# First stage of a transformer layer: buffers for h's rows, later weight parts, table products on GpSimd, and more summed z

## The reference, cut to what matters

```python
dt = jnp.exp(log_dt)
dt_Lambda = dt[:, None, 0] * Lambda[None, :, 0] + 1j * (dt[:, None, 1] * Lambda[None, :, 1])
pos = jnp.arange(L, dtype=jnp.float32)            # L = 1024
...
num = jnp.exp(dt_Lambda_neg) - 1
den = jnp.exp(dt_Lambda_neg * L) - 1
Wc = Wc * num * _reciprocal(den * Lam, EPS)       # Wc is x, as complex numbers
P = dt_Lambda[..., None] * pos - P_max[..., None]
K = jnp.einsum('chn,hnl->chl', Wc, jnp.exp(P))
return K.real.astype(jnp.float32)
...
h = _L0_tok_ref(L0_tok_log_dt, L0_tok_Lambda, x, 1024)
h = h + _L0_attn_ref(_layernorm(h, axis=-1), L0_attn_Wq, L0_attn_Wk, L0_attn_Wv, L0_attn_Wo)
h = h + _L0_ffn_ref(_layernorm(h, axis=-1), L0_ffn_A, L0_ffn_B, L0_ffn_Wr, L0_ffn_br)
```

## Time and profile before

| | |
|---|---|
| time, median of 3 runs | 2504.96 us (2502.73 to 2509.3) |
| the profiled execution's own time | 2504.22 us, span 2502.4 us |
| first stage, its first matmul to its last | 42.06 to 294.94 us |
| TensorE busy over the span | 2349.1 us (94%) |
| VectorE, ScalarE, GpSimd busy over the span | 1952.3, 1850.1, 1629.6 us |
| second stage, from its first load | 300.40 us to the end |

### The profile page before, as it was taken

One profiled execution on the slowest core, in us unless ns is written; L12 is line 12 of the kernel. 1 busy time (PEld: TensorE's weight loads), 2 busy tenths in 40 slices (PEclk: granted clock), 3 DMA queues, 4 the chain that ended last, 5 costly groups with the idle time before them and its releaser, 6 DMA issues.

```text
span 2502.4 us, 58994 instructions
## 1 busy us (share of the span) xinstructions
PE 2349.1 (94%) x18752; PEld 1245.7 (50%) x18752; DVE 1952.3 (78%) x7939; ACT 1850.1 (74%) x6398; POOL 1629.6 (65%) x1508
## 2 busy tenths in 40 slices
PE   2888679999999999999999999999999999999986
PEld 2677534444455544454455454444555545444543
DVE  8888547888788778788787778788887778887864
ACT  5777547777777777777777777777777777777773
POOL 1233147777777777777777777777777777777772
PEclk9999889999999999999999999999999999999997
DMA  2777559999999999999999999999999999999984
GB/s 74 215 210 213 166 103 167 176 184 184 182 186 188 183 177 179 186 185 184 181 188 186 185 174 181 185 185 184 184 187 184 179 181 182 184 186 186 182 164 101
DMA packets 1199527, 443.66 MB, mean 177 GB/s; under 512 B 1149552, under 2 KB 1151856, under 8 KB 1199216
## 3 DMA queue, kind: packets, MB, share of 16 engines
q1 hardware_dynamic: 1199216, 439.89, 88.9%
HBM read 87.42 MB, written 67.11 MB: 62 GB/s over the span
## 4 chain that ended last, share of the span: by engine, by line
PE 69%; DVE 13%; issue 2%; ACT 2%; POOL 1%; DMA 1%; POOLq 0%; DVEq 0%; ACTq 0%
PE pb L817 8%; PE pb L819 7%; PE pb L818 7%; PE pa L817 6%; PE pa L818 6%; PE pa L819 6%; PE pv_ps L846 4%; PE pc L817 4%; PE pc L818 4%; PE pc L819 4%; PE s_ps L831 4%; DVE pr L1111 2%; DVE bn L1130 2%; DVE h L1221 2%; DVE nrm L1144 2%
## 5 line engine op out<-in xcount | busy, mean ns | idle before, releaser
L968 ACT ACTIVATE pr<-pr,smin 128x128 f32<-128x128 f32 x2048 | 792.8, 389 | 111.5 <-DVE smin L1111 111.3
L1325 POOL TENSOR_TENSOR p<-pr,p 128x512 f16<-128x512 f32 x512 | 600.8, 1174 | 254.1 <-ACT p L978 244.0
L1317 POOL TENSOR_TENSOR pr<-pr,rinv 128x512 f32<-128x512 f32 x512 | 529.7, 1040 | 268.2 <-DVE rinv L1119 268.2
L978 ACT ACTIVATE p<-pr 128x512 f16<-128x512 f32 x512 | 319.6, 624 | 238.5 <-POOL pr L1317 218.6
L1111 DVE CUSTOM_DVE_ANT_0 pr<-s_ps,cst 128x128 f32<-128x128 f32 x2048 | 470.3, 284 | 27.0 <-POOL p L1325 13.9
L968 ACT ACTIVATION_READ_ACCUMULATOR pr<-pr,smin 128x1 f32 x2048 | 383.6, 187 | 0.0
L576 PE MATMUL hps<-z,xw 128*128 128x256 f32 x896 | 214.5, 402 | 80.4 <-POOL xw L304 42.1
L576 PEld LDWEIGHTS hps<-z,xw 128*128 128x128 f32 x896 | 179.8, 203 | 114.7 <-issue 45.8
L831 PEld LDWEIGHTS s_ps<-kt,qt 128*128 128x128 f16 x2048 | 152.7, 98 | 145.3 <-DVE smin L1111 45.4
L1165 DVE TENSOR_TENSOR xs<-h_ln,xs 128x512 f16<-128x512 f32 x128 | 123.7, 968 | 125.1 <-ACT xs L1013 125.1
L817 PE MATMUL pa<-wkv_hi,xt 128*128 128x512 f16 x512 | 197.2, 385 | 25.0 <-DMA xt<-xs 25.0
(11 more groups left out here) (189 smaller groups left out, 5747.1 us busy)
## 6 DMA issues: line engine op xcount, KB each, us to landing
h<-hout SPq DMA_DIRECT2D x128, 256.0 KB, 3.3
h_ln<-h SPq DMA_DIRECT2D x64, 512.0 KB, 4.3
h_res<-h SPq DMA_DIRECT2D x64, 512.0 KB, 4.7
out<-h SPq DMA_DIRECT2D x64, 512.0 KB, 5.4
pt<-p SPq DMA_TRANSPOSE x512, 3.3
xa<-x SPq DMA_DIRECT2D x16, 256.0 KB, 4.7
xb<-x SPq DMA_DIRECT2D x32, 128.0 KB, 4.0
wst<-wq SPq DMA_DIRECT2D x8, 512.0 KB, 5.3
```

The costliest lines, as they stand in the source:

```text
L968: last = A.activation(p, p, ACT.Exp, bias=smin[g % 2][:, j:j + 1], scale=-1.0, accum_out=rsum[g % 2][:, j:j + 1])
L978: A.activation(p16[g % 2][:, 0:HG * P], pr[g % 2][:, :], ACT.Copy).then_inc(ph_done, 1)
L1317: nc.gpsimd.tensor_tensor(p3, p3, rinv[g % 2][:, :].unsqueeze(2).broadcast_to([P, HG, P]), ALU.mult).then_inc(p_norm, 1)
L1325: nc.gpsimd.tensor_tensor(p[:, HG * P:], pr[g % 2][:, :], p[:, 0:HG * P], ALU.subtract).then_inc(pl_done, 1)
```

## The change

The third buffer of h's rows (HR = 3); all z of the last chunk are summed, both of a window after both are made; the weight parts: wo is due in window 2 of the chunk, aw and bm in window 0 of the next, wq and wkv where they were; ScalarE makes a high part at the end of the window before the due one, behind the evictions, and VectorE makes a low part at the end of its window, behind the table step. For all chunks but the first, three products move from VectorE to GpSimd: the first product of `angles`, the sines' product of `tables`, the first product of `digits`; each stands behind an `add` in GpSimd's queue. They are counted by `tab_p` (3 a chunk), and `tab_v` counts 10.

```diff
-HR = 2
+HR = 3
...
-        TV, TA = 13, 3
+        TV, TA, TP = 10, 3, 3
...
         def summed(g):
-            return g % 2 == 1 and g // 2 % PER_CHUNK in SUM_AT
+            return g // (TC // 2) == CHUNKS - 1 or g % 2 == 1 and g // 2 % PER_CHUNK in SUM_AT
...
-            PIECES += [(4 * k + 1, "wq", k, D, 1), (4 * k + 1, "wo", k, D, 1)]
+            PIECES += [(4 * k + 1, "wq", k, D, 1), (4 * k + 2, "wo", k, D, 1), (4 * k + 3, "wkv", k, 512, 2)]
             if k < 2:
-                PIECES.append((4 * k + 2, ("aw", "bm")[k], None, (KC * AW, D)[k], 1))
-            PIECES.append((4 * k + 3, "wkv", k, 512, 2))
+                PIECES.append((4 * k + 4, ("aw", "bm")[k], None, (KC * AW, D)[k], 1))
...
+        def first_angles(eng, k):
+            return eng.tensor_tensor(theta[:, :, :], across(zi, k, NPOS),
+                                     pos[:, :].unsqueeze(1).broadcast_to([P, TC, NPOS]), ALU.mult)
+
+        def table_i(eng, k):
+            return eng.tensor_tensor(tab[k % 2][:, :, 1, :], expo[:, k * TC:k * TC + TC, :], theta[:, :, :], ALU.mult)
+
+        def digits_m1(eng, k):
+            return eng.tensor_tensor(dm1[:, :, :].rearrange("p t (s n) -> p t s n", s=2), across(rr, k, 2, DIG),
+                                     tab[k % 2][:, :, :, 0:DIG], ALU.mult)
...
+                pool.wait_ge(pre_v, N_PRE)
                 for w in range(WINDOWS):
                     add(w)
+                    k, at = (w - 1) // PER_CHUNK, (w - 1) % PER_CHUNK
+                    if w >= 1 and k + 1 < CHUNKS:
+                        if at == 0:
+                            pool.wait_ge(tab_v, TV * k + 10)
+                            first_angles(nc.gpsimd, k + 1).then_inc(tab_p, 1)
+                        if at == 2:
+                            pool.wait_ge(tab_a, TA * (k + 1) + 2)
+                            pool.wait_ge(z_made, k * (TC // 2))
+                            table_i(nc.gpsimd, k + 1).then_inc(tab_p, 1)
+                        if at == 3:
+                            pool.wait_ge(tab_v, TV * (k + 1) + 7)
+                            pool.wait_ge(tab_p, TP * (k + 1) + 2)
+                            digits_m1(nc.gpsimd, k + 1).then_inc(tab_p, 1)
...
                     k = w // PER_CHUNK
                     if w % PER_CHUNK == 1 and k + 1 < CHUNKS:
                         sines(k + 1)
-                    for n, piece in enumerate(PIECES):
-                        if w == (piece[0] - 1 if piece[1] == "wq" else piece[0]):
-                            weight_hi(n)
                     for e in range(WIN):
                         if e < ON_ACT and w + LEAD < WINDOWS:
                             products(w + LEAD, e)
                         evict(WIN * w + e)
+                    for n, piece in enumerate(PIECES):
+                        if piece[0] == w + 1:
+                            weight_hi(n)
...
-                    table_z(2 * w)
-                    table_z(2 * w + 1)
+                    for g in (2 * w, 2 * w + 1):
+                        table_z(g)
                     if w == 0:
                         swapped(1)
-                    if at in SUM_AT:
-                        sum_z(2 * w + 1)
-                    for n, piece in enumerate(PIECES):
-                        if piece[0] == w:
-                            weight_lo(n)
+                    for g in (2 * w, 2 * w + 1):
+                        if summed(g):
+                            sum_z(g)
                     if k + 1 < CHUNKS:
                         if at == 0:
                             angles(k + 1)
...
                         if at == 3:
                             digits(k + 1)
+                    for n, piece in enumerate(PIECES):
+                        if piece[0] == w:
+                            weight_lo(n)
```

More of the change, by code:

```diff
@@ L211, in s4_stage @@
         tab_a = sem("tab_a")
+        tab_p = sem("tab_p")
         pr_done = sem("pr_done")
@@ L246, in weight, with across @@
             return t[:, :, :].rearrange("p k n -> p (k n)") if name.startswith("aw") else t[:, :]
+        def across(row, k, *shape):
+            a = row[:, k * TC:k * TC + TC].unsqueeze(2)
+            return a.broadcast_to([P, TC, shape[0]]) if len(shape) == 1 else \
+                a.unsqueeze(3).broadcast_to([P, TC, *shape])
+        def first_angles(eng, k):
[6 more added lines that the diff above has]
+                                     tab[k % 2][:, :, :, 0:DIG], ALU.mult)
         with nc.Block() as block:
@@ L295, in _ @@
                 for i in range(HR):
-                    sp.wait_ge(h_sent[i], 32 * (T // 2 // HR))
+                    sp.wait_ge(h_sent[i], 32 * len(range(i, T // 2, HR)))
             @block.gpsimd
@@ L412, in tables, with digits @@
                     V.tensor_scalar(half[:, :, :], half[:, :, :], -2.0, 1.0, ALU.mult, ALU.add).then_inc(tab_v, 1)
-                    V.tensor_tensor(at[:, :, 1, :], expo[:, toks, :], theta[:, :, :], ALU.mult).then_inc(tab_v, 1)
-                    dve.wait_ge(tab_v, TV * k + 7)
-                    V.tensor_tensor(at[:, :, 0, :], expo[:, toks, :], half[:, :, :], ALU.mult).then_inc(tab_v, 1)
-                def digits(k):
-                    at = tab[k % 2][:, :, :, 0:DIG]
-                    m1, m2 = (a[:, :, :].rearrange("p t (s n) -> p t s n", s=2) for a in (dm1, dm2))
-                    dve.wait_ge(tab_v, TV * k + 9)
-                    V.tensor_tensor(m1, across(rr, k, 2, DIG), at, ALU.mult).then_inc(tab_v, 1)
-                    V.tensor_tensor(m2, across(ss, k, 2, DIG), at, ALU.mult).then_inc(tab_v, 1)
-                    dve.wait_ge(tab_v, TV * k + 11)
+                    if k == 0:
+                        table_i(V, k).then_inc(tab_p, 1)
+                    dve.wait_ge(tab_v, TV * k + 6)
+                    V.tensor_tensor(tab[k % 2][:, :, 0, :], expo[:, k * TC:k * TC + TC, :], half[:, :, :],
+                                    ALU.mult).then_inc(tab_v, 1)
+                def digits(k):
+                    m1, m2 = (a[:, :, :].rearrange("p t (s n) -> p t s n", s=2) for a in (dm1, dm2))
+                    dve.wait_ge(tab_v, TV * k + 7)
+                    dve.wait_ge(tab_p, TP * k + 2)
+                    if k == 0:
+                        digits_m1(V, k).then_inc(tab_p, 1)
+                    V.tensor_tensor(m2, across(ss, k, 2, DIG), tab[k % 2][:, :, :, 0:DIG], ALU.mult).then_inc(tab_v, 1)
+                    dve.wait_ge(tab_v, TV * k + 8)
+                    dve.wait_ge(tab_p, TP * k + 3)
                     V.tensor_tensor(u4[k % 2][:, :, 0, :], m1[:, :, 0, :], m2[:, :, 1, :], ALU.add).then_inc(tab_v, 1)
@@ L449, in table_z @@
                     if at == 0:
[L450 removed]
+                        dve.wait_ge(tab_v, TV * k + 10)
+                        dve.wait_ge(tab_p, TP * k + 2)
                     digit = u[k % 2][:, :].rearrange("p (s n) -> p s n", n=DIG)[:, 4 * at:4 * at + 4, :]
@@ L537, in _ @@
                 step(V.scalar_tensor_tensor(rr[:, :], gr, re_row, t0, ALU.mult, ALU.subtract))
+                assert steps[0] == N_PRE
                 tables(0)
```

24 lines of the change are left out of this document (9 added, 15 removed).

## The result

The changed kernel takes 2479.52 us (median of four runs, 2476.65 to 2481.44), the kernel before, on the same chip, 2506.36 (2502.73 to 2509.3). The ratio is 0.9893, 95% interval 0.9875 to 0.991: 1.1% faster. The profiled execution has a span of 2478.4 us, 24.0 less than before.

The account below looks back on a forecast made before the run. The prediction took VectorE's queue, work plus waits, to set the first stage's period; -35.2 + 4.0 + 10.9 - 4.3 = -24.6 us from 2504.2 gave 2479.6, with a range of 2465 to 2495.

Parts of the forecast that it names:

- Waits gone, -35.2: First stage up to the last chunk: VectorE's waits for ScalarE's high weight parts vanish, -35.2 of 41.2 us.
- a new wait, +4.0: VectorE waits 1.0 us before wo_lo in the four chunks without aw or bm, +4.0 us; bounds 0 to 2 a chunk.
- window A: First of a chunk's four windows: TensorE's lower clock after idling adds 1.6 us; angles behind GpSimd's product cost VectorE +0.6.
- ScalarE's waits for the stores nearly gone: First stage, third buffer for h: ScalarE's 29.8 us of store waits fall to at most 1 us left in places.
- Rival 3: Third buffer brings nothing because stores are issued late; waits for wkv_hi return: 2491 to 2499 us, chance 0.06.
- Products on GpSimd, +10.9: Three table products on GpSimd block VectorE's steps: +1.5 us a chunk for six chunks, +1.9 in the first, +10.9.
- B and C: Second and third window of a chunk: in C, GpSimd's sines' product delays VectorE's cosines' product, +0.4 us.
- D: Last of a chunk's four windows: VectorE's digit product waits for GpSimd's, +0.5 us.
- Last chunk, -4.3: Last chunk of the first stage, every z summed: VectorE sets the time, 27.8 us become 23.5, -4.3; bounds -2 and -5.
- Second stage, 0: Way into the second stage and that stage itself: no changed instruction, so 0 us.
- Rival 2: First stage: the wait moves to another weight part, wo_lo waiting 3 us in six chunks: +14, 2494 us, chance 0.12.
- Rival 4: GpSimd's three products cost far more; gain gone at 2.3 us each, 2519 us in all at 3.0: chance 0.05.

Follow-up runs that it names:

- the matmuls of constants: The changed kernel plus eight matmuls of constants into an unread PSUM bank ahead of TensorE's first and third window of the last chunk: 2476.78 us.
- the products alone: The kernel before with only the three table products moved to GpSimd, two buffers, weight parts and last chunk as before: 2510.23 us, ratio 1.0019.

## Why the prediction was right

The forecast was 2479.6 us for the profiled execution, which took 2480.2. Its terms, step by step:

- **Waits gone, -35.2, and a new wait, +4.0: -31.2 up to the last chunk's start.** The run with the products on VectorE has this part alone: its last chunk starts at 234.24, before at 267.17, -32.9. Right: it has 2.2 us of new waits before wo_lo, so -35.1 without them. The new wait of the changed kernel is smaller than written and mostly in another place: up to the last chunk it is 3.1 us (wo_lo 1.08, 0.27, 0.28; wq_lo 0.82 and 0.69), and the wo_lo wait of 1.08 is in the first chunk, which the prediction had left out. The lower clock was expected at every window A. It came in two of six, the fourth and seventh chunk: after 1.95 us of idle time 56 records took 14.01 us for 12.32, and it was wq_hi that came late. After the same idle time in the second, third, fifth and sixth chunk the records took 0.22 us each, at a granted clock of 1.00. The last section has the rows. The split of the term between its two causes was not seen: with the weight parts early the buffer alone takes 14.6 us, and with them late it takes 5.9.
- **ScalarE's waits for the stores nearly gone:** no row is left, where up to 1 us in places was allowed. Rival 3 falls.
- **Products on GpSimd, +10.9:** 9.6, of which 0.9 are the longer waits for weight parts (3.1 us for 2.2), so 8.7 in the sense of the sum. Ahead of the add, where nothing blocks them, the first product and the digit product take 1.05 us and the sines' product, which writes every other half row, 1.28 (1.1 taken for all three). A chunk without waits for weights takes 27.91 us (186.75 to 214.66), before 26.9: +1.0, not +1.5, and with the waits 27.9 to 29.2, where 28.4 to 29.4 was written. By windows: A 7.80 for 7.35, +0.45 (+0.6 taken); B and C 12.74 for 12.35, +0.39 (+0.4); D 7.37 for 7.22, +0.15 (+0.5). The first chunk came out as worked: L421 starts at 47.18 (47.3 was written). D was priced too high: its base is 7.22, not 7.1, and GpSimd's product is done 5.51 us after the window's start, not 5.7. In C and D the order is as written: VectorE's step goes first, the halving step in C and the sum in D. On record GpSimd's product starts right behind the add nonetheless, with its wait inside: 1.47 and 1.50 us, so the block works both ways. By the Trainium skill, SBUF — State Buffer, section "SBUF: two separate sides", such a lock is held for a whole instruction; the rows agree, L441 ending only 0.55 us behind GpSimd's product.
- **Last chunk, -4.3:** -0.4, outside the bounds (-2 to -5). The step that failed is "VectorE sets the time, then 8 records, 1.8". From the chunk's start VectorE's last sum ends after 22.8 us, not 21.7: its work is 21.2 us, close to what was written, and 1.53 us is a wait before wq_lo, the mishap named in the bounds. Then TensorE needs 4.6 us more, not 1.8, since from 261.65 on it has 32 records at 0.30 us: 9.56 us, where 0.22 gives 7.0. That is 2.5 us by the clock. The prediction had shown the lower clock after an idle time and priced it for window A, and left it out here, where it made TensorE idle more. That the clock took it is shown by the matmuls of constants, which bring back 2.4 us.
- **Second stage, 0:** 2201.65 for 2202.0.

Predicted up to the last chunk -20.3, measured -23.3; in it -4.3 and -0.4. Two errors of 3 and 4 us with opposite signs meet in a sum that is right to 1 us. The runs confirm that the waits go and that the products cost time by the block; the clock's effect was wrong in window A and in the last chunk. That the total is that close is chance.

Rival 2 had the right kind (another weight part, 0.12) but a size of 14 us where 3 were seen. Rival 4 needed a product of over 2.3 us; they are 1.05 to 1.28.

What the parts add up to, each on top of the one before, in the first stage: third buffer -14.6 (300.40 to 285.80); products on GpSimd and the last chunk's sums +1.6 (287.41); later weight parts -10.7 (276.75). The products cost only that little while the weight parts are early: VectorE's waits for wkv_hi and wo_hi fall by 5 us at that step, so part of what the products take was idle time anyway.

## What to carry to other kernels

Ask of a product that moves from VectorE to GpSimd not whether GpSimd is idle but what VectorE does in the same microsecond. Behind an add and beside a table step it cost 9.6 us; the same product ahead of the add, beside operations that don't block, is part of a kernel 14 us faster. Two repairs of one wait don't add up: price each with the other in place. Halving an engine's work needn't shorten it: the idle time that this opens can lower its clock. For such a stretch price both durations that the rows show, here 0.22 us a record and 0.28 to 0.30, and don't take the better one.

## What the runs showed of the hardware

**A waiting instruction of one engine lengthens in the record, on either side.** GpSimd's digit product reads 1.05 us ahead of the add and 1.50 where VectorE's sum goes first; VectorE's second product L441 reads 0.68 alone and 1.65. Between two products back to back VectorE is let in once (1.64 us in the run with the product made twice).

**The same idle time can be followed by either clock.** TensorE in the changed kernel, at the start of the third chunk and of the seventh:

```profile
103.04 7.14 PE L608 MATMUL hps<-z,xw 128*128 128x256 f32 x32 [1.95 <-issue]
...
217.44 14.01 PE L608 MATMUL hps<-z,xw 128*128 128x256 f32 x56 [1.95 <-issue]
```

The first stretch has a granted clock of 1.00, 0.22 us a record, the second 0.88, 0.25. In the kernel before, 3.33 us of idle time ahead of 72.23 were followed by 24 records at 0.23 us, and 3.36 us ahead of 237.85 by the slow ones of the earlier trace rows. What decides between them is not shown here.

**Unchanged code can run into the same block.** Two runs, the last chunk summed as before and the products alone, have a second stage of 2208.25 and 2209.2 us, 6.6 more than the changed kernel and 7.2 more than the kernel before, with no instruction of it changed. In the other eleven kernels it takes 2200.1 to 2203.7 us. In both, and not in the kernels before and after, the waits between 500 and 2400 us have these rows, here of the first:

```profile
PE pb L849 <- DVE rt_s L1209: 5.0, 4, 1.2
...
DVE pr L1143 <- issue: 0.7, 4, 0.2
```

and the timeline of VectorE at one of the four places:

```profile
1055.47 0.29 DVE L1143 CUSTOM_DVE_ANT_0 pr<-s_ps,cst 128x128 f32<-128x128 f32 x1 [0.19 <-issue]
...
1056.11 0.75 DVE L1176 SCALAR_TENSOR_TENSOR nrm<-nrm 128x1 f32<-128x1 f32 x1
...
1057.08 0.98 DVE L1180 TENSOR_TENSOR nrm<-nrm 128x1 f32<-128x1 f32 x1
```

The same steps of the changed kernel:

```profile
1055.96 0.34 DVE L1176 SCALAR_TENSOR_TENSOR nrm<-nrm 128x1 f32<-128x1 f32 x1
...
1056.53 0.46 DVE L1180 TENSOR_TENSOR nrm<-nrm 128x1 f32<-128x1 f32 x1
```

A gap of 0.19 us at issue comes ahead of steps on one number a row. In the changed kernel L1176 reads 0.21 to 0.74 us over the stage and L1180 0.16 to 0.47; here they read 0.75 and 0.98, beside GpSimd's operations, together 0.93 more than in the same place of the changed kernel. TensorE waits 1.2 us for what follows. Four such places make 5.0 of the 6.6 us. That the gap shifts these steps against GpSimd's is read from the rows and not tested. Why it arises in these two kernels is open: the code there is the same in all, and no run was made on it. It means that a change of the first stage can't be judged by the kernel's time alone: these two lost 6.6 and 7.2 us where nothing was changed.
